# Mixture of experts with results sent to their tokens' places by indirect stores, read back in order, and summed on TensorE

## The reference, cut to what matters

```
h = layernorm(x)                                  # per token, no gain
p = h @ gate_w                                    # 8 logits; the best two experts e1, e2
g1, g2 = softmax of the two best logits
r(e) = gelu(layernorm(h @ w1[e] + b1[e]) * ln1_g[e] + ln1_b[e]) @ w2[e] + b2[e]
s = h + g1 * r(e1) + g2 * r(e2)
out = layernorm(layernorm(s) * ln_g + ln_b) + x
```

## Time and profile before

| what | us |
|---|---|
| median of 3 runs | 4227.38 |
| the runs | 4233.18, 4219.45, 4227.38 |
| the profiled execution's own time | 4227.27 |
| its span in the profile | 4225.5 |
| busy in the span: PE / DVE / ACT / POOL | 3640.5 / 2420.3 / 1748.9 / 1582.0 |
| the last result of a block is written | 4057.3 |

### The profile page before, as it was taken

One profiled execution on the slowest core, in us unless ns is written; L12 is line 12 of the kernel. 1 busy time (PEld: TensorE's weight loads), 2 busy tenths in 40 slices (PEclk: granted clock), 3 DMA queues, 4 the chain that ended last, 5 costly groups with the idle time before them and its releaser, 6 DMA issues. The chain is left out here.

```text
span 4225.5 us, 59934 instructions
## 1 busy us (share of the span) xinstructions
PE 3640.5 (86%) x17328; PEld 2176.8 (52%) x17328; DVE 2420.3 (57%) x6561; ACT 1748.9 (41%) x3994; POOL 1582.0 (37%) x1718
## 2 busy tenths in 40 slices
PE   6999999999689998998999989769999999569940
PEld 3556655556445555554555556434555554446620
DVE  6676776767466663234565523436666665455557
ACT  2544554445345554112555521125555555124410
POOL 2343433433367664002766622421222221442244
PEclk8999999999799999999999999969999999679975
DMA  6565765557201102453010122222222221269942
GB/s 104 69 80 66 94 86 82 77 62 91 59 31 50 50 35 70 164 202 119 26 50 35 38 74 70 62 72 63 57 57 67 57 57 44 104 199 319 317 152 70
DMA packets 230321, 377.77 MB, mean 89 GB/s; under 512 B 39822, under 2 KB 166098, under 8 KB 223698
## 3 DMA queue, kind: packets, MB, share of 16 engines
q1 hardware_dynamic: 218770, 356.77, 35.6%
q0 software_dynamic: 6144, 16.79, 1.2%
q10 hardware_dynamic: 5184, 1.58, 0.2%
HBM read 170.03 MB, written 84.93 MB: 60 GB/s over the span
## 5 line engine op out<-in xcount | busy, mean ns | idle before, releaser
L758 DVE CUSTOM_DVE_ANT_0 a_ps<-a_ps,a_mask 128x128 f32<-128x128 f32 (+3 forms) x1024 | 479.9, 512 | 194.1 <-PE a_ps L513 176.3
L2479 ACT ACTIVATE c_probsT<-c_ps 128x512 f32<-128x512 f32 x512 | 298.6, 600 | 335.4 <-PE c_ps L2301 326.2
L368 POOL TENSOR_SCALAR_AFFINE_SELECT a_probs_c<-a_probs_c 128x256 f32<-128x256 f32 (+1 forms) x384 | 187.4, 504 | 664.6 <-ACT a_probs_c L663 664.4
L2618 DVE TENSOR_REDUCE c_neg_max<-c_ps 128x1 f32<-128x512 f32 x512 | 337.1, 684 | 160.4 <-PE c_ps L2289 159.0
L663 ACT ACTIVATE a_probs_c<-a_ps 128x512 f32<-128x512 f32 x640 | 344.9, 603 | 100.0 <-PE a_ps L531 75.0
L513 PE MATMUL a_ps<-a_packed_qk 65*128 65x128 f32 (+3 forms) x1024 | 338.3, 374 | 47.3 <-DVE a_maxima L758 26.8
L1094 POOL TENSOR_TENSOR w_probs<-w_probs,w_inv 128x1024 f32<-128x1024 f32 x128 | 242.3, 1893 | 334.8 <-DVE w_inv L1457 334.8
L549 PE MATMUL a_ps<-a_probs_c,a_v 128*64 128x512 f32 (+3 forms) x2048 | 316.6, 453 | 1.0 <-POOL a_probs_c L368 0.8
L531 PE MATMUL a_ps<-a_packed_qk 67*128 67x512 f32 (+3 forms) x1024 | 288.5, 344 | 1.6 <-DMA a_packed_qk<-a_max_half 1.5
L2289 PE MATMUL c_ps<-c_packed_qk 68*128 68x512 f32 x512 | 256.1, 506 | 10.5 <-DVE c_neg_max L2618 6.6
L1349 ACT ACTIVATE w_probs<-w_ps_s,w_neg_max 128x256 f32<-128x256 f32 x512 | 235.9, 478 | 66.9 <-DVE w_neg_max L1452 66.2
(11 more groups left out here) (323 smaller groups left out, 7723.5 us busy)
## 6 DMA issues: line engine op xcount, KB each, us to landing
a_packed_qk<-a_halves SPq DMA_DIRECT2D x512, 128.0 KB, 4.6
d_w<-in_L_ffn_second SPq DMA_DIRECT2D x71, 516.0 KB, 4.9
d_w<-in_L_ffn_first SPq DMA_DIRECT2D x71, 512.0 KB, 5.0
rows_dram<-f_zeros SPq DMA_DIRECT2D x8, 4096.0 KB, 15.7
c_packed_qk<-c_halves SPq DMA_DIRECT2D x256, 128.0 KB, 2.3
w_v<-w_v_next SPq DMA_DIRECT2D x16, 1024.0 KB, 4.6
d_rows<-rows_dram SPq DMA_DIRECT2D x71, 128.0 KB, 4.2
mixed_dram<-d_y SPq DMA_DIRECT2D x71, 128.0 KB, 4.8
```

The lines of the kernel that those rows point to most:

```text
L758: last = nc.vector.tensor_tensor_reduce(tile, tile, mask[:, (NT - 1 - i) * P:], 1.0, -3e38, ALU.add, ALU.max, accum_out=maxima_of[:, hd // ...
L2479: nc.scalar.activation(probsT[:, q % 2, r, :], ps_again[u % 2][:, :], ACT.Exp).then_inc(exp_done.sem, 1)
L2618: nc.vector.tensor_reduce(neg_max[:, g % 2, 0, s % GS:s % GS + 1], bank("s", s)[:, :], AX.X, ALU.max, negate=True).then_inc(max_ready.sem, 1)
```

## The change

Each row of `h` becomes 258 floats: column 0 is the place of the token (512 + 2 x token number), columns 1 to 256 the values, column 257 the number of the second expert. The scatter carries them with the row, so that each block's rows hold their own places. In the block loop POOL compares a row's second expert with the block's expert, adds the place (`find_goals`, two blocks ahead), replaces rows of padding by spare places below 512, and sends the 128 results by one indirect DMA to `mixed_dram` (`send`), which now is in the order of tokens with a token's two results side by side. SP's `store` is gone, the first four loads of w1 go ahead of the wait for the scatters, and rows are a load of their own. In the last phase SP reads 1 MB a batch with plain DMAs into three buffers; ACT multiplies the two results by their weights in place (`weigh`); PE adds h and both by multiplying with the identity into PSUM (`sum_results`), four batches in rotation; DVE takes statistics from PSUM, scales with `ln_g` and `ln_b` and takes statistics again, one batch behind; POOL makes the roots and -mean x root; ACT applies them (`norm_output`, two batches behind); POOL adds `x` (`add_input`, two batches behind) and ACT issues the store (three batches behind).

The diff, cut to its core:

```diff
@@ third stage and tables @@
-        zeros = sb("zeros", [P, 8 * D])
+        zeros = sb("zeros", [P, 8 * (D + 2)])
...
+    con["goals"] = places.reshape(36, 128).T.astype(np.float32)
@@ sync @@
+            def load_rows(j):
+                if j >= HOLD:
+                    sp.wait_ge(goal_added.sem, goal_added.at(j - HOLD, 1))
                 row = sp.value_load(plan[0:1, 1, j:j + 1], min_val=0, max_val=SPARE)
                 sp.dma_start(rows[:, j % HOLD, :], sorted_dram[bass.ds(row, P), :]).then_inc(rows_in[j % HOLD].sem, 16)
...
-            def store(j):
-                sp.wait_ge(y_ready.sem, y_ready.at(j, 1))
-                sp.dma_start(mixed_dram[j * P:(j + 1) * P, :], y[:, j % HOLD, :]).then_inc(y_stored[j % HOLD].sem, 16)
-
             sp.wait_ge(plan_ready.sem, 1)
+            for j in range(HOLD):
+                load_first(j)
             sp.wait_ge(sorted_in.sem, sorted_in.at(B, 0))
-            for s in range(BLOCKS + 8):
+            for s in range(BLOCKS + 2):
+                if HOLD <= s < BLOCKS:
+                    load_first(s)
                 if s < BLOCKS:
-                    load_first(s)
+                    load_rows(s)
                 if 0 <= s - 2 < BLOCKS:
                     load_second(s - 2)
-                if 0 <= s - 7 < BLOCKS:
-                    store(s - 7)
-
+
+            def load_results(b):
+                if b >= 3:
+                    sp.wait_ge(sum_psum.sem, sum_psum.at(b - 3, 1))
+                lo = HOLD * P + 2 * b * N
+                sp.dma_start(got[:, b % 3, :, :, :], mixed_dram[lo:lo + 2 * N, :].rearrange("(t p k) d -> p t k d", p=P, k=2))\
+                  .then_inc(got_in[b % 3].sem, 16)
+
+            for i in range(HOLD):
+                sp.wait_ge(y_stored[i].sem, y_stored[i].at((BLOCKS - 1 - i) // HOLD, 16))
             for b in range(B):
-                sp.wait_ge(out_ready.sem, out_ready.at(b, 1))
-                sp.dma_start(out_v[b], acc[:, b % 2, :, :]).then_inc(stored[b % 2].sem, 16)
+                load_results(b)
@@ gpsimd @@
+            def find_goals(j):
+                if j == 0:
+                    pool.wait_ge(plan_ready.sem, 1)
+                pool.wait_ge(rows_in[j % HOLD].sem, rows_in[j % HOLD].at(j // HOLD, 16))
+                to = slice(j % GOALS, j % GOALS + 1)
+                nc.gpsimd.tensor_scalar(goal_f[:, to], rows[:, j % HOLD, D + 1:D + 2], expert_f[:, j:j + 1],
+                                        rows[:, j % HOLD, 0:1], ALU.is_equal, ALU.add).then_inc(goal_added.sem, 1)
...
+            def send(j):
+                pool.wait_ge(y_ready.sem, y_ready.at(j, 1))
+                pool.wait_ge(goal_ready.sem, goal_ready.at(j, 1))
+                if j >= HOLD:
+                    pool.wait_ge(y_stored[j % HOLD].sem, y_stored[j % HOLD].at(j // HOLD, 0))
+                nc.gpsimd.indirect_dma_start(
+                    mixed_dram[:, :], bass.IndirectOffsetOnAxis(ap=goal[:, j % GOALS:j % GOALS + 1], axis=0),
+                    y[:, j % HOLD, :], None).then_inc(y_stored[j % HOLD].sem, 16)
...
-            for j in range(BLOCKS):
-                roots.step(pool, j, 0, rstd[:, j % 2, :], mv[:, j % 2, 1:2], EPS, neg_half[:, 0:1])
...
+            for s in range(BLOCKS + 3):
+                if s < BLOCKS:
+                    roots.step(pool, s, 0, rstd[:, s % 2, :], mv[:, s % 2, 1:2], EPS, neg_half[:, 0:1])
+                if 0 <= s - 3:
+                    send(s - 3)
+                if s + 2 < BLOCKS:
+                    find_goals(s + 2)
...
+            for s in range(B + 2):
+                if s < B:
+                    root_of_sum(s)
+                if 0 <= s - 1 < B:
+                    root_of_output(s - 1)
+                if s >= 2:
+                    add_input(s - 2)
@@ tensor @@
+            def sum_results(b):
+                if b >= 4:
+                    pe.wait_ge(scaled_once.sem, scaled_once.at(b - 4, 1))
+                elif b == 3:
+                    pe.wait_ge(y_ready.sem, y_ready.at(BLOCKS, 0))
+                for k in range(-1, 2):
+                    if k >= 0:
+                        pe.wait_ge(weighted.sem, weighted.at(b, k + 1))
+                    for t in range(NT):
+                        last = nc.tensor.matmul(sums(b, t), ident[:, :], h[b][:, t, 1:D + 1] if k < 0 else got[:, b % 3, t, k, :],
+                                                start=k < 0 and t % 2 == 0, stop=k == 1 and t % 2 == 1)
+                last.then_inc(sum_psum.sem, 1)
@@ scalar @@
+            def weigh(b, k):
+                act.wait_ge(got_in[b % 3].sem, got_in[b % 3].at(b // 3 + 1, 0))
+                for t in range(NT):
+                    last = nc.scalar.activation(got[:, b % 3, t, k, :], got[:, b % 3, t, k, :], ACT.Identity,
+                                                scale=pair[:, b, k, t:t + 1])
+                last.then_inc(weighted.sem, 1)
...
+            for s in range(B + 3):
+                if s < B:
+                    weigh(s, 0)
+                    weigh(s, 1)
+                if 0 <= s - 2 < B:
+                    norm_output(s - 2)
+                if s >= 3:
+                    store(s - 3)
@@ vector @@
-            for b in range(B):
-                collect(b)
-                finish(b)
+            for s in range(B + 1):
+                if s < B:
+                    sum_stats(s)
+                if s >= 1:
+                    scale_output(s - 1)
+                    output_stats(s - 1)
```

205 lines of the change are left out of this document (114 added, 91 removed).

## The result

| | before | changed |
|---|---|---|
| median of the runs, us | 4228.47 (4 runs) | 4168.85 (4 runs) |
| lowest to highest | 4219.45 to 4233.18 | 4161.97 to 4171.13 |
| profiled execution, span | 4225.5 | 4166.9 (time 4168.6) |
| last result ready to the end | 168.2 | 108.9 |
| first multiplication of block 0 to last result | 299.6 | 299.9 |

The ratio of the times is 0.9859 [0.9839, 0.9879]: 59.6 us faster, where some 72 were forecast (4155.0, range 4138 to 4178). The direction and the place were right. The terms for the clock and for the end were too small, a link was missing, and of two smaller gains, 2.5 and 1.5 us, this profile shows next to nothing.

The account below looks back on a forecast made before the run. TensorE bounds the block loop at 4.10 us a block; afterwards VectorE and GpSimd work in turn. The last-phase chain gave 4148.9, plus 4.3 end and 4 clock, less 2.5 and 1.5, plus 1.8 around the span: 4155.0 us, range 4138 to 4178.

Parts of the forecast that it names:

- The likeliest case with its unit costs: Whole kernel: the main forecast of 4155 us, 4141 to 4168 with its unit costs, chance 0.60.
- the rival of a cold TensorE: Last phase: TensorE stays at 1.2 GHz, 10.4 us a batch, and becomes the bound; 4170 us, chance 0.15.
- the signs named: Checks: last phase 97 to 100 us, VectorE's cadence 8.5 to 9.5, block period 4.10, rows 1 taken before 3755.2.
- the first sum: Last phase: send landing, 1 MB load, weighing 1.9 us, TensorE passes 2.9 and 1.8 us; sum 0 at 4071.9.
- the two turns of the loop: Last phase: two batches take 17.6 us through VectorE, GpSimd, ScalarE and TensorE, counted twice; 8.8 us a batch instead of 18.8.
- the 4.0 set aside for the clock: Last phase: every second batch meets about 2.7 us at half rate, 1.4 us lost; 4 us in all, 0 to 19.
- the last step: Last phase, after the loop: 9.7 us given without terms, then VectorE's step without sum statistics, 5.4 us, to 4141.8.
- The end: Last phase: root and shift 2.15, two additions 4.8, store issue 0.1, then 4.3 us to the span's end.
- Unit costs: Last phase: prices per operation taken from profile rows, such as VectorE's step 7.2 us and GpSimd's addition 2.43 us.
- Start of the blocks: Before block 0: early weight loads let rows 1 leave two slots earlier; 2.5 us less, between 0 and 3.3.
- Block loop: Block loop: SP loses one DMA, loads leave about 0.4 us earlier, TensorE waits less for rows; 1.5 us less, 0 to 2.7.
- Rivals on DMA: Block loop: DMA becomes the bound, 4170 us, chance 0.13; or sends land too late, slower than before, chance 0.03.

Follow-up runs that it names:

- late weights: Changed kernel with the first four weight loads put back behind the wait for the scattered rows; 4163.41 us, ratio 0.9853.
- the two undisturbed profiles: Two variants of the changed kernel: last-phase stores on SP instead of ScalarE, 4157.44 us; sends and plain loads with the old last phase, 4208.58 us.

## Why the prediction was right, and where it was off

Its direction rests on one reading, that VectorE and GpSimd took turns over 150 us and much of VectorE's work could go. That held: VectorE's busy time there fell from 107.9 to 58.1 us. The likeliest case with its unit costs was given as 4141 to 4168, and the measured 4168.85 lies just above it; the stated range, up to 4178, was made wider for the rival of a cold TensorE and for DMA. Of the signs named, two did not come: the last phase is 108.9 us, not 97 to 100, and a batch takes 10.0 us, not 8.5 to 9.5. The profiled span of 4166.9 us is 13.7 above the 4153.2 forecast: 9.1 in the last phase, and 4.6 in the last result, which comes at 4057.97 instead of 4053.35.

- *Last phase, 99.9 forecast, 108.9 measured: +9.1.* By its parts: the first sum +1.9 (16.4 us after the last result instead of 14.6, its two passes mostly at half rate), from there to sum 3 +4.5, the two turns of the loop +5.2, less the 4.0 set aside for the clock, the last step -0.9 (its 9.7 stands in the sum without terms), the end +2.5.
- *The clock.* The step said that every second batch meets "about 2.7 us at half rate, 1.4 us lost", from a rise 2.3 us after work began. In the loop the passes of batches 3, 5 and 7 ran at half rate for their first 4.7, 5.5 and 5.9 us and took 6.03, 6.43 and 6.63 instead of 3.62: 8.2 us lost, twice the term. The waits ahead of them were 6.0 to 6.7 us, not 4.3. The 2.3 us also count only from the multiplications of block 0. TensorE had turned rows 0 before them, 5.7 us ahead of the rise:

```profile
3754.26 0.69 PE L3042 MATMUL d_ps_h<-ident,d_rows 128*128 128x128 f32 x2 [22.47 <-DMA d_rows<-rows_dram]
```

  The mechanism was right, the size off. The Trainium skill's remark on bursts that each start cold (TensorE: Matmul & The Clock Gate, HAM oscillation) fits: each odd batch is such a burst. The rival of a TensorE cold throughout gives nearly the measured time, 4170, but is not what happened: the even batches' passes took 3.6 to 3.7 us, TensorE idled 6 us before each odd one and was not the bound.
- *The link through ScalarE's queue.* The loop was traced through GpSimd's addition and ScalarE's store. That path is real, but ScalarE's normalisation runs beside the addition and stands ahead of the weighing too. The stretch from sum 1 to sum 3, forecast as two steps of VectorE, has this link already: ScalarE took up batch 3's weighing only at 4090.69, behind a normalisation that waited for a shift. This and the half-rate passes of batch 3, 6.03 us, are the +4.5. With store and normalisation both out of the way 14.2 us go.
- *The end.* "4.3 us to the span's end" was read off a kernel whose last operation was VectorE's. With the last addition on GpSimd its drain comes behind: 2.9 us.
- *Unit costs.* VectorE's step 6.95 (7.2), root to shift 2.10 (2.15), addition 2.35 (2.43), weighings 3.30 (3.8), four passes of ScalarE with scale and shift 2.07 (1.87), from the first load's issue to the first weighing 5.5 (5.1), send landed 2.4 after issue in the variants that show it (2.7): right within 0.5 us each. VectorE's second scaling, priced at 1.68 from a row with an idle GpSimd, took 2.6 to 3.8 where GpSimd added beside it. The Trainium skill's 6.15 us for 1 MB (DMA: Bandwidth & Descriptors, Measured) is above the first load's 5.5. The third of the three loads that left together landed 10.3 us after its issue, a later one alone 5.3, and nothing waited for them after the first.
- *Start of the blocks, -2.5 forecast.* Real at block 0 in an undisturbed execution: 8.7 and 8.8 us after the last scatter instead of 11.2, though the early weights do share DMA with the last scatters, against the forecast. A part is given back at once. TensorE begins to turn rows 1.6 us before its first multiplication, where it was 3.5, and the granted clock rises later behind that multiplication. Here are three of the microseconds behind the one at 3758.07, of the changed kernel:

```profile
3760.07:3761.07 1.00, 1.00 (x3) 0.40 (x2) 0.00 (x0) 0.00 (x0) 0.00 (x0) 0.50 1.06 276
3762.07:3763.07 1.00, 1.00 (x3) 0.50 (x3) 0.97 (x2) 0.37 (x1) 0.00 (x0) 0.72 0.04 17
3763.07:3764.07 1.00, 1.00 (x4) 0.34 (x3) 0.51 (x2) 0.00 (x0) 0.22 (x1) 1.00 0.65 127
```

  It is still 0.50 there after 2 us and comes up in the fifth; before it came up in the third, and with late weights too. With early weights it took 3.8 to 5.0 us, some 2 us more at half rate, an estimated 1 us of the 2.4: the first four blocks take 14.2 us in the two undisturbed profiles, 13.2 before. So from the last scatter to block 4 it takes 24.4 us before, 24.5 with late weights, 23.0 in those two: 1.4 us are kept of the 2.5. What hid them in the times to the last result is the next point, late rows in the loop, which vary by more than that from profile to profile. In the change's own profiles the standstill costs another 1.1 to 1.6 us at block 0, and to block 4 it takes 24.4 and 23.9. The forecast took the start for a pure shift.
- *Block loop, -1.5 forecast.* It took 1.5 off TensorE's 2.7 us of waiting for rows, counting on rows that leave 0.4 us earlier. Late rows cost more than that wait, 4.6 us before, and the change left 4.0 of them in one profile and 7.8 in the other: no gain that can be told from their spread. The DMA that SP loses was not what made rows late. They stood behind 512 KB of weights.
- *Rivals on DMA.* The share stayed at 0.93 to 0.95, so the sends did not fill it, nor did rows of 1032 bytes. What the Trainium skill says of a descriptor off a 256-byte boundary (DMA: Bandwidth & Descriptors, How a descriptor splits into AXI transactions) would not have moved the sum, and nothing here contradicts it. In the profile of the change VectorE never waited for a send.

## What to carry over

When a loop runs through an in-order queue, list everything that stands ahead of the next useful instruction, not only the last of it: removing the store alone gave 3 us, and putting the work that does not wait first as well gave 14. A cover that hides one term may be as long as the term: ask what is next in the queue before taking the whole off. In a queue shared by big and small transfers, send the small one that is wanted first ahead: a change of order and one more wait gave 4 us or more. A row of waits names the price of a late transfer only in part; the period of the loop shows all of it.

## What was not expected of the hardware

- GpSimd's closing drain ended 5.9 us after its last operation, whether an addition of 2.35 us or a shift of 0.20 (5.3 us before the change), and the span did not end before it. With the last addition on VectorE the end came 4 us sooner.
- A VectorE operation with both operands in SBUF was held until a GpSimd addition with operands in SBUF had ended: 2565 ns instead of 479, 5.86 us instead of 1.67 for four.
- VectorE stood still between instructions of its own, 0.5 to 2.5 us at a time, in the routing of 8 of 13 profiled executions of the change and its variants, all but possibly the first on one chip. The cause stays open.
- Executions of one kernel on one chip differ by 5 to 22 us, so a piece of 3 us can be judged only by a stretch within a profile.
